# Softmax sums in a decoder kernel: from the exponentials' accumulator to matmuls with a block of ones

## The chip, the cores and the metric

The kernel runs on one core of one Trainium2 chip. The metric is device time of one execution in microseconds (us), as the median of the runs. The engines are TensorE (PE in the rows, its weight loads PEld), VectorE (DVE), ScalarE (ACT), GpSimd (POOL) and the DMA queue of SyncE (SP).

## The reference, cut to what matters

A decoder block on 32 sequences of 128 tokens, width 128, in fp32: a selective state-space layer (scan), then masked attention to a second input with 16 heads of width 8, then a mixture of 8 experts, each followed by a layer norm. The change lies in the attention:

```
scores = jnp.einsum('bnhd,bmhd->bhnm', q, k) / sqrt(8)     # then pad and causal mask
attn = jax.nn.softmax(scores, axis=-1)
out = jnp.einsum('bhnm,bmhd->bnhd', attn, v).reshape(b, s, d)
return out @ Wo.T + bo
```

The softmax is computed as exp(score - max), summed over the keys, and the division is done after the product with the values.

## The kernel before, in words

The 32 sequences go through in G = 8 groups of S = 4. For a group `g` the scan layer runs in a loop of 16 units (`entries` on TensorE, `decay` on ScalarE, `states` on VectorE, `times_c` on GpSimd, `y_add` on TensorE), with pieces of the group before (`w`) and the two after (`e`, `c`) woven in by hand. Behind the loop comes the attention stage of the group, with `t` = 0 to 3 for its four sequences. After the eighth group a routing table is built and 72 expert tiles and a last norm follow. Every engine has one instruction stream, written out in order; an instruction waits on semaphores with `at(engine, name, count)`.

One sequence `t` of the attention stage goes like this.

- `scores(g, t, k)`: TensorE writes the mask and then q times k for 16 heads in four PSUM banks, heads 0 to 7 with k = 0 and 8 to 15 with k = 1 (L1477 the masks, L1484 the products).
- `maxima(g, t, k)`: VectorE takes the negative maxima (L974), two instructions for each half.
- `exps(g, t, k)`: ScalarE takes the exponentials, one instruction for each head, into `prob`, and each also accumulates its row sum into `den` (L692). The trace shows an ACTIVATION_READ_ACCUMULATOR behind each ACTIVATE.
- `head_t(g, t, c)`: TensorE transposes the four heads of block c (L1495) into bank 6 or 7, and `pT_out` copies them to SBUF: c = 0 and 2 on ScalarE (L702), c = 1 and 3 on VectorE (L989).
- `heads_v(g, t)`: 16 matmuls of the transposed exponentials with `v_block` (L1518), in four column blocks of 32, so that head dimensions lie on rows and queries on columns.
- The inverse sums: `inverses` takes the reciprocal of 16 sums for each query (L979), `widen` repeats each 8 times (L983 on VectorE, L706 on ScalarE for t = 3), `inverses_t` transposes the result on TensorE (L1504), it is copied to `rdenT` (L994 on VectorE, L711 on ScalarE for t = 3), and `normed` multiplies (L999) into `aoT`.
- `second_out` projects `aoT` with Wo (L1527, L1529).

`inverses_t(g, t-1)` and `heads_v(g, t-1)` stand in TensorE's stream in turn `t`, between `scores(g, t+1, 0)` and `head_t(g, t, 0)`; those of t = 3 stand behind `entries(e, 1)`. In the turn t = 3 the first two units of the next group are begun: `entries(e, 0)`, `entries(e, 1)`, `decay`, `states(e, 0)` and `states(e, 1)` stand among the last transposes and copies. `entries(e, 2)` stands behind `second_out`, since it writes the bank pair in which `aoT`'s input lies.

Of the kernel before, what the change touches and what calls it, by code (L numbers as in the profile page):

```python
# [8 lines left out]
ALU = mybir.AluOpType  # L9
# [35 lines left out]
def build(nc, a, out):  # L45
    ctx = ExitStack()
    with ctx:
# [20 lines left out]
        sum32 = sb("sum32", [P, 32])  # L68
        diag64 = sb("diag64", [P, HK])
# [66 lines left out]
        rden_wide = sb("rden_wide", [P, 2, P])  # L136
# [3 lines left out]
        den = sb("den", [P, 2, H])  # L140
# [8 lines left out]
        rden = sb("rden", [P, 2, H])  # L149
# [75 lines left out]
        pad_sb mask_sb s_ps s_neg p_sb rden_sb rden_wide_sb pT_ps pT_sb pTd_sb pv_ps rdenT_ps rdenT_sb rdenTd_sb aoT_sb wo_ps  # L225
# [201 lines left out]
        def _(pool):  # L427
# [32 lines left out]
            link(g_.memset(v_block[:, :, :, :], 0.0))  # L460

# [109 lines left out]
        def _(act):  # L571
# [110 lines left out]
            def exps(g, t, k):  # L682
                if t < 2:
                    at(act, "y_sum", 4 * g + 3 + t)
                else:
                    at(act, "pT_ps", 16 * g + 4 * (t - 2) + 2 * k + 2)
                    at(act, "rden_sb", S * g + t - 1)
                for h in range(8 * k, 8 * k + 8):
                    c, j = divmod(h, 4)
                    if j == 0:  # L690
                        at(act, "s_neg", 16 * g + 4 * t + c + 1)
                    last = A(prob[:, t % 2, c, j, :], bank[2 + c][:, j * L:(j + 1) * L], ACT.Exp, bias=nmax[:, t % 2, h:h + 1],  # L692
                             accum_out=den[:, t % 2, h:h + 1])
# [9 lines left out]

            def widen(g, t):
                at(act, "rden_sb", S * g + t + 1)
                A(rden_wide[:, t % 2, :].rearrange("p (h d) -> p h d", h=H), rden[:, t % 2, :].unsqueeze(2).broadcast_to((P, H, HD)),  # L706
                  ACT.Copy).then_inc(s["rden_wide_sb"], 1)

            def rdenT_out(g, t):
                at(act, "rdenT_ps", S * g + t + 1)  # L710
                A(rdenT[:, t % 2], bank[(t + 1) % 2][:, 2 * P:3 * P], ACT.Copy).then_inc(s["rdenT_sb"], 1)  # L711
# [36 lines left out]
            for m in range(G):  # L748
# [55 lines left out]
                for t in range(S):  # L804
                    pT_out(g, t, 0)
                    if t == S - 1:
                        if e is not None:
                            decay(e, 0, range(2))
                        widen(g, t)
                        if e is not None:  # L810
                            decay(e, 0, range(2, NQ))
# [5 lines left out]
                if e is not None:  # L817
                    decay(e, 1, range(2))
                rdenT_out(g, S - 1)
                if e is not None:  # L820
                    decay(e, 1, range(2, NQ))
# [55 lines left out]
        def _(dve):  # L877
# [99 lines left out]
            def inverses(g, t):  # L977
                at(dve, "p_sb", 16 * g + 4 * t + 4)
                v_.reciprocal(rden[:, t % 2, :], den[:, t % 2, :]).then_inc(s["rden_sb"], 1)  # L979

            def widen(g, t):
                at(dve, "rden_sb", S * g + t + 1)
                TT(rden_wide[:, t % 2, :].rearrange("p (h d) -> p h d", h=H), rden[:, t % 2, :].unsqueeze(2).broadcast_to((P, H, HD)),  # L983
                   one_col[:, :].unsqueeze(2).broadcast_to((P, H, HD)), ALU.mult).then_inc(s["rden_wide_sb"], 1)
# [6 lines left out]
            def normed(g, t):  # L991
                if t < S - 1:
                    at(dve, "rdenT_ps", S * g + t + 1)
                    v_.tensor_copy(rdenT[:, t % 2], bank[(t + 1) % 2][:, 2 * P:3 * P]).then_inc(s["rdenTd_sb"], 1)  # L994
                    at(dve, "rdenTd_sb", (S - 1) * g + t + 1)
                else:
                    at(dve, "rdenT_sb", g + 1)
# [77 lines left out]
            for m in range(G):  # L1075
                w, e, c = parts(m)
                g = m
                if w is not None:
                    normed(w, S - 1)
                    second_stats(w, range(S - 1))  # L1080
# [34 lines left out]
                for t in range(S):  # L1115
                    if t == S - 1 and w is not None:
                        ranked(w)
                        normed(g, t - 1)
# [4 lines left out]
                    inverses(g, t)  # L1123
# [646 lines left out]
```

## Time and profile before

| | us |
|---|---|
| median of 3 runs | 1138.08 |
| lowest and highest run | 1131.46, 1140.45 |
| the profiled execution, its own time | 1135.38 |
| span of its profile | 1133.5 |

In the profile PE is busy 962.6 us, ACT 720.5, DVE 697.1 and POOL 576.0. Times in rows are counted from the start of the span. A row of a timeline has the start, the length, the engine, the line and operation, output and inputs, shapes and the count of merged instructions, and in brackets how long the engine was idle before it and what released it. An idle time of 0 is not printed. Lengths overlap: the next instruction of an engine often starts before the modelled end of the one before, so that what one costs is read from start to start.

### The profile page before, as it was taken

The numbers are of one execution on the slowest core, as the hardware profiler recorded it, in microseconds if no ns is written. First come the engines' busy times: TensorE is split into PE (matmuls) and PEld (weight loads), VectorE is DVE, ScalarE is ACT, GpSimd is POOL, SyncE is SP. The second block draws the span as 40 slices with busy tenths as digits, with TensorE's granted clock in tenths as the row PEclk, the third lists the DMA queues.
The fourth block names the chain that finished last, engine by engine and source line by source line (L and its number), as shares of the span: only waits on it lengthen the run. The fifth ranks groups of instructions, "written<-read, shape, count | busy, mean of one in ns | idle before, by whom it ended". The sixth has DMA issues, their size and how long they took to land.

```text
span 1133.5 us, 28078 instructions
## 1 busy us (share of the span) xinstructions
PE 962.6 (85%) x9703; PEld 543.2 (48%) x9704; DVE 697.1 (62%) x1371; ACT 720.5 (64%) x2212; POOL 576.0 (51%) x395
## 2 busy tenths in 40 slices
PE   6799889989788888979888885976937999999997
PEld 2344544444354445435444542543434666666662
DVE  0467667786577767657766794796653544444437
ACT  3567966876696677669667882964822444444446
POOL 2578258457726954782696388268041333333320
PEclk9889999999899999989999996998977999999999
DMA  4606104201500520050042005003131111111134
GB/s 113 138 15 132 30 1 96 66 2 38 133 12 4 124 54 3 17 136 28 4 107 60 4 16 137 2 4 118 50 119 44 41 41 42 42 42 42 42 105 151
DMA packets 69227, 66.69 MB, mean 59 GB/s; under 512 B 9728, under 2 KB 63104, under 8 KB 68736
## 3 DMA queue, kind: packets, MB, share of 16 engines
q1 hardware_dynamic: 63856, 55.59, 19.8%
q0 software_dynamic: 4352, 8.99, 2.4%
q8 instruction: 69, 1.13, 0.4%
q10 hardware_dynamic: 912, 0.67, 0.2%
q14 instruction: 38, 0.31, 0.1%
HBM read 49.09 MB, written 16.13 MB: 58 GB/s over the span
## 4 chain that ended last, share of the span: by engine, by line
PE 45%; POOL 21%; issue 20%; ACT 8%; DVE 5%; DMA 1%; SPq 0%; POOLq 0%; DVEq 0%; ACTq 0%
POOL hst L494 8%; PE pair_a L1682 6%; PE pair_b L1683 6%; PE bank L1696 6%; POOL prob L494 6%; ACT prob L692 5%; POOL xg L526 4%; PE y_ps L1404 3%; PE y_ps L1688 3%; PE pair_b L1484 3%; PE bank L1302 2%; PE y_ps L1484 2%; PE bank L1495 2%; PE pair_a L1518 2%; PE pair_a L1382 1%
## 5 line engine op out<-in xcount | busy, mean ns | idle before, releaser
L651 ACT ACTIVATE decays<-w,a_neg 128x256 f32<-128x256 f32 x512 | 220.5, 509 | 30.2 <-DVE hst L920 17.6
L494 POOL TENSOR_TENSOR hst<-hst,c_rep 128x1024 f32<-128x1024 f32 x64 | 151.4, 2372 | 73.8 <-DVE hst L920 73.1
L494 POOL TENSOR_TENSOR prob<-prob,c_rep 128x1024 f32<-128x1024 f32 x56 | 133.2, 2381 | 57.3 <-DVE prob L920 56.7
L566 POOL DMA_INDIRECT y<-aoT,dest x72 | 69.6, 966 | 173.2 <-DVE aoT L1232 168.8
L920 DVE TENSOR_TENSOR_SCAN prob<-decays,pair_b 128x1024 f32<-128x1024 f32 x32 | 73.1, 2284 | 69.4 <-issue 54.6
L692 ACT ACTIVATE prob<-pair_b,nmax 128x128 f32<-128x128 f32 x256 | 90.4, 399 | 22.4 <-DVE nmax L974 22.3
L1191 DVE TENSOR_TENSOR zpos<-zabs,pair_b 128x512 f32<-128x512 f32 x74 | 50.8, 687 | 81.3 <-PE pair_b L1683 80.2
L1404 PE MATMUL y_ps<-hst,sum 128*32 128x256 f32 x512 | 74.4, 442 | 24.4 <-POOL prob L494 24.4
L692 ACT ACTIVATE prob<-y_ps,nmax 128x128 f32<-128x128 f32 x256 | 90.8, 415 | 0.0
L526 POOL DMA_INDIRECT xg<-x_all,pos x64 | 64.8, 1013 | 35.8 <-DVE pos L1066 23.7
L920 DVE TENSOR_TENSOR_SCAN prob<-decays,pair_a 128x1024 f32<-128x1024 f32 x32 | 73.0, 2281 | 13.5 <-ACT decays L651 9.9
L1682 PE MATMUL pair_a<-w,qk 128*128 x148 | 77.7, 607 | 0.5 <-ACT qk L829 0.5
L1683 PE MATMUL pair_b<-w,qk 128*128 x148 | 76.5, 599 | 0.0
L1696 PE MATMUL bank<-prob,decays 128*128 x576 | 76.1, 275 | 0.0
L1495 PE MATMUL bank<-ident,prob 128*128 128x128 f32 x512 | 70.7, 279 | 5.3 <-ACT pT L702 5.3
L846 ACT ACTIVATE decays<-y_ps 128x512 f32<-128x512 f32 x72 | 43.0, 598 | 50.2 <-PE y_ps L1688 49.5
L1404 PE MATMUL y_ps<-prob,sum 128*32 128x256 f32 x512 | 74.5, 442 | 0.0
L1382 PE MATMUL pair_b<-w,du_tok 64*32 64x256 f32 x2048 | 72.1, 390 | 2.4 <-DVE prob L920 2.3
L486 POOL TENSOR_TENSOR w<-diag,b_tok 128x1024 f32<-128x1024 f32 x32 | 60.6, 1925 | 26.3 <-ACT b_tok L633 26.3
L920 DVE TENSOR_TENSOR_SCAN hst<-decays,pair_b 128x1024 f32<-128x1024 f32 x32 | 72.6, 2270 | 1.6 <-PE pair_b L1382 1.6
L833 ACT ACTIVATE zabs<-pair_a 128x512 f32<-128x512 f32 x74 | 44.2, 597 | 45.4 <-PE pair_a L1682 45.4
L1302 PE MATMUL bank<-xT,w_conv 128*128 128x512 f32 x112 | 62.1, 676 | 10.1 <-ACT xT L581 10.1
(281 smaller groups left out, 2186.0 us busy)
## 6 DMA issues: line engine op xcount, KB each, us to landing
w<-d_dram SPq DMA_DIRECT2D x64, 256.0 KB
c_rep<-c_dram SPq DMA_DIRECT2D x64, 128.0 KB, 3.4
qk<-xg SPq DMA_DIRECT2D x79, 65.0 KB, 1.9
d_dram<-zpos SPq DMA_DIRECT2D x8, 512.0 KB, 3.0
xn<-in_x SPq DMA_DIRECT2D x8, 256.0 KB, 3.0
cn<-in_ctx SPq DMA_DIRECT2D x8, 256.0 KB, 3.3
mask_b<-in_mask SPq DMA_DIRECT2D x8, 256.0 KB, 3.4
w<-in_w1T SPq DMA_DIRECT2D x1, 2048.0 KB, 8.4
```

What stands on the lines that cost most here:

```text
L494: g_.tensor_tensor(by_state(ring(k)), by_state(ring(k)), c_rep[:, :, toks[r]].rearrange("p q (i t) -> p i q t", i=2), ALU.mult).then_inc(s ...
L526: pool.indirect_dma_start(xg[:, :], bass.IndirectOffsetOnAxis(ap=pos[:, t, k:k + 1], axis=0), x2_all[:, w * S + t, :], None).then_inc(s["s ...
L651: last = A(by_state(decays[:, k % 2, :])[:, :, q, :], delta_rep[:, b, toks[r]].rearrange("p (i t) -> p i t", i=2), ACT.Exp, scale=a_neg[:, ...
L692: last = A(prob[:, t % 2, c, j, :], bank[2 + c][:, j * L:(j + 1) * L], ACT.Exp, bias=nmax[:, t % 2, h:h + 1], accum_out=den[:, t % 2, h:h ...
L920: v_.tensor_tensor_scan(ring(k), decays[:, k % 2, :], pair(k)[:, :, :].rearrange("p i c -> p (i c)"), 0.0, ALU.mult, ALU.add).then_inc(s[" ...
L1302: last = MM(bank[b].rearrange("p (s t) -> p s t", s=S), w_conv[:, k, h * P:(h + 1) * P], xT[:, :, k:k + L], start=(k == 0), stop=(k == KCO ...
L1382: last = MM(pair(k)[32 * j:32 * j + 32, i, :].rearrange("p (q y t) -> p q y t", q=NQ, y=2)[:, :, y, :], du_tok[half, r, y, 32 * b:32 * b + ...
L1404: last = MM(y_ps[32 * i:32 * i + 32, r, h * HT:(h + 1) * HT].rearrange("p (i t) -> p i t", i=2), sum32[:, :], by_state(ring(4 * x + i))[:, ...
L1495: last = TR(bank[6 + c % 2][:, j * L:(j + 1) * L], prob[:, t % 2, c, j, :], ident[:, :])
L1682: MM(bank[b], xsT[:, b, :], w1[:, bass.ds(e, 1), :].rearrange("p a f -> p (a f)"), start=True, stop=True).then_inc(s["up_ps"], 1)
L1683: MM(bank[2 + b], xsT[:, b, :], w3[:, bass.ds(e, 1), :].rearrange("p a f -> p (a f)"), start=True, stop=True).then_inc(s["up_ps"], 1)
L1696: last = MM(bank[6][:, b * P:(b + 1) * P], gT[:, b, c, :], w2[:, bass.ds(e, 1), c, :].rearrange("p a d -> p (a d)"), start=(c == 0), stop= ...
```

## The change

The exponentials no longer accumulate. A constant `ones_block` [128, 4, 32] has ones in columns 8j to 8j+7 of block j; `sums_of` multiplies the same transposed exponentials that `heads_v` reads with it, in 16 matmuls of the same shapes, so that each sum stands in PSUM on the 8 rows of its head's values, where `rdenT` wants it. VectorE takes the reciprocal of that 128x128 block straight from PSUM into `rdenT`. `widen`, `inverses_t`, the copy to `rdenT` and the 128x16 reciprocal go, with `den`, `rden` and `rden_wide`. In VectorE's stream `inverses(g, t-1)` now stands directly ahead of `normed(g, t-1)`, that of t = 3 at the start of the next group's loop.

```diff
+        ones_block = sb("ones_block", [P, 4, 32])
...
             link(g_.memset(v_block[:, :, :, :], 0.0))
+            link(g_.memset(ones_block[:, :, :], 0.0))
+            for j in range(4):
+                link(g_.memset(ones_block[:, j, j * HD:(j + 1) * HD], 1.0))
...
# exps (ScalarE)
                     at(act, "pT_ps", 16 * g + 4 * (t - 2) + 2 * k + 2)
-                    at(act, "rden_sb", S * g + t - 1)
...
-                    last = A(prob[:, t % 2, c, j, :], bank[2 + c][:, j * L:(j + 1) * L], ACT.Exp, bias=nmax[:, t % 2, h:h + 1],
-                             accum_out=den[:, t % 2, h:h + 1])
+                    last = A(prob[:, t % 2, c, j, :], bank[2 + c][:, j * L:(j + 1) * L], ACT.Exp, bias=nmax[:, t % 2, h:h + 1])
...
# ScalarE, order of the attention stage
-                    if t == S - 1:
-                        if e is not None:
-                            decay(e, 0, range(2))
-                        widen(g, t)
-                        if e is not None:
-                            decay(e, 0, range(2, NQ))
+                    if t == S - 1 and e is not None:
+                        decay(e, 0, range(NQ))
...
# VectorE
             def inverses(g, t):
-                at(dve, "p_sb", 16 * g + 4 * t + 4)
-                v_.reciprocal(rden[:, t % 2, :], den[:, t % 2, :]).then_inc(s["rden_sb"], 1)
+                at(dve, "den_ps", S * g + t + 1)
+                v_.reciprocal(rdenT[:, t % 2], bank[(t + 1) % 2][:, 2 * P:3 * P]).then_inc(s["rdenT_sb"], 1)
...
                 if w is not None:
+                    inverses(w, S - 1)
                     normed(w, S - 1)
...
-                    inverses(g, t)
-                    if t + 1 < S:
-                        widen(g, t)
                     if t and not (t == S - 1 and w is not None):
+                        inverses(g, t - 1)
                         normed(g, t - 1)
...
# TensorE
-            def inverses_t(g, t):
-                at(pe, "rden_wide_sb", S * g + t + 1)
+            def sums_of(g, t):
+
+                at(pe, "pT_sb", 8 * g + 2 * t + 2)
+                at(pe, "pTd_sb", 8 * g + 2 * t + 2)
                 if t:
                     at(pe, "aoT_sb", S * g + t)
                 else:
                     at(pe, "rotq_sb", 4 * g + 4)
-                TR(bank[(t + 1) % 2][:, 2 * P:3 * P], rden_wide[:, t % 2, :], ident[:, :]).then_inc(s["rdenT_ps"], 1)
+                for j in range(4):
+                    for c in range(4):
+                        last = MM(bank[(t + 1) % 2][32 * c:32 * c + 32, 2 * P:3 * P], ones_block[:, j, :], pT_half[c // 2][:, c % 2, j, :],
+                                  start=(j == 0), stop=(j == 3), skip_group_check=True)
+                last.then_inc(s["den_ps"], 1)
```

## Rows read from the trace of the kernel before

**Rows 1.** The page: busy time by engine, and the chain by engine.

```profile
PE 962.6 (85%) x9703; PEld 543.2 (48%) x9704; DVE 697.1 (62%) x1371; ACT 720.5 (64%) x2212; POOL 576.0 (51%) x395
...
PE 45%; POOL 21%; issue 20%; ACT 8%; DVE 5%; DMA 1%; SPq 0%; POOLq 0%; DVEq 0%; ACTq 0%
```

**Rows 2.** Windows: length, busy PE, PEld, DVE, ACT, POOL, granted clock, DMA share, GB/s.

```profile
408.00:420.00 12.00, 11.47 (x84) 6.14 (x82) 10.34 (x34) 10.14 (x53) 5.13 (x4) 1.00 0.15 44
420.00:431.00 11.00, 9.99 (x84) 5.68 (x83) 8.62 (x21) 10.50 (x54) 1.27 (x1) 1.00 0.11 26
```

**Rows 3.** Timeline of TensorE, attention stage of one group, t = 0 to 2.

```profile
411.05 1.04 PE L1495 MATMUL bank<-ident,prob 128*128 128x128 f32 x8
412.62 0.70 PE L1464 MATMUL pair_a<-aoT,wqT 128*128 128x256 f32 x2 [0.53 <-ACT aoT L680]
...
418.54 0.33 PE L1504 MATMUL pair_a<-ident,rden_wide 128*128 128x128 f32 x1
418.80 0.30 PE L1518 MATMUL pair_a<-pT,v_block 128*32 128x128 f32 x2
...
419.59 0.28 PE L1518 MATMUL pair_a<-pT,v_block 128*32 128x128 f32 x2
...
419.81 1.09 PE L1495 MATMUL bank<-ident,prob 128*128 128x128 f32 x8
420.74 0.59 PE L1477 MATMUL y_ps<-mbias,identb 128*128 128x512 bf16 x2
...
423.25 0.38 PE L1477 MATMUL pair_b<-mbias,identb 128*128 128x512 bf16 x1
423.95 0.39 PE L1477 MATMUL pair_b<-mbias,identb 128*128 128x512 bf16 x1 [0.32 <-ACT prob L692]
424.27 1.13 PE L1484 MATMUL pair_b<-hst,qk 32*128 32x512 f32 x4
...
427.53 0.59 PE L1477 MATMUL y_ps<-mbias,identb 128*128 128x512 bf16 x2
428.05 1.13 PE L1484 MATMUL y_ps<-hst,qk 32*128 32x512 f32 x4
```

**Rows 4.** Timeline of TensorE, the same stage, t = 3 and behind it.

```profile
431.23 0.30 PE L1518 MATMUL pair_a<-pT,v_block 128*32 128x128 f32 x2 [0.91 <-ACT hst L702]
...
434.60 0.63 PE L1495 MATMUL bank<-ident,prob 128*128 128x128 f32 x4 [0.57 <-ACT pT L702]
...
439.39 0.30 PE L1518 MATMUL pair_a<-pT,v_block 128*32 128x128 f32 x2 [1.26 <-issue]
...
441.88 0.46 PE L1527 MATMUL bank<-x1b,ident 128*128 128x128 f32 x2
```

**Rows 5.** Timeline of ScalarE, the same stage.

```profile
411.80 0.40 ACT L692 ACTIVATE prob<-y_ps,nmax 128x128 f32<-128x128 f32 x1
412.05 0.24 ACT L692 ACTIVATION_READ_ACCUMULATOR prob<-y_ps,nmax 128x1 f32 x1
412.14 0.42 ACT L680 ACTIVATE aoT<-pair_a 128x256 f32<-128x256 f32 x1
...
433.75 0.71 ACT L702 ACTIVATE pT<-bank 128x512 f32<-128x512 f32 x1
```

**Rows 6.** Timeline of VectorE, end of the stage and start of the next group.

```profile
430.42 0.68 DVE L989 COPY hst<-bank 128x512 f32<-128x512 f32 x1
...
438.62 0.67 DVE L989 COPY hst<-bank 128x512 f32<-128x512 f32 x1
...
443.75 2.29 DVE L920 TENSOR_TENSOR_SCAN prob<-decays,pair_a 128x1024 f32<-128x1024 f32 x1 [1.04 <-PE pair_a L1382]
```

**Rows 7.** Groups of VectorE by line and shape: busy us, mean ns.

```profile
L979 DVE RECIPROCAL rden<-den 128x16 f32<-128x16 f32 x32 | 8.1, 252 | 9.2 <-ACT prob L692 9.2
...
L1253 DVE RECIPROCAL gates_all<-hst 128x64 f32<-128x64 f32 x1 | 0.6, 553 | 0.0
```

**Rows 8.** Timeline of TensorE, first group, t = 3, answering to 434.60.

```profile
139.45 0.63 PE L1495 MATMUL bank<-ident,prob 128*128 128x128 f32 x4 [1.27 <-ACT pT L702]
```

More of the change, by code:

```diff
@@ L135, in build @@
         rdenT = sb("rdenT", [P, 2, L])
-        rden_wide = sb("rden_wide", [P, 2, P])
         pad = sb("pad", [P, T])
@@ L139, in build @@
         nmax = sb("nmax", [P, 2, H])
-        den = sb("den", [P, 2, H])
         prob = sb("prob", [P, 2, 4, 4, L])
@@ L148, in build @@
                   hst[:, 2, :], hst[:, 3, :], prob_u[:, 2, :], prob_u[:, 3, :]]
-        rden = sb("rden", [P, 2, H])
         aoT = sb("aoT", [P, T])
@@ L224, in build @@
         ln1_stat ln1_var ln1_log ln1_rstd x1_sb x1b_sb x1T_ps x1T_sb cT_ps cT_sb k_ps rotk_sb k_sb k_heads_sb v_ps v_sb q_ps rotq_sb q_sb
-        pad_sb mask_sb s_ps s_neg p_sb rden_sb rden_wide_sb pT_ps pT_sb pTd_sb pv_ps rdenT_ps rdenT_sb rdenTd_sb aoT_sb wo_ps
+        pad_sb mask_sb s_ps s_neg p_sb pT_ps pT_sb pTd_sb pv_ps den_ps rdenT_sb aoT_sb wo_ps
         ln2_stat ln2_var ln2_log ln2_rstd x2_sb x2T_ps x2T_sb lg_ps lg_sb route rank_ps pos_sb row_sb scat
@@ L702, in pT_out @@
                 A(pT_half[c // 2][:, 0], bank[6].rearrange("p (j q) -> p j q", j=4), ACT.Copy).then_inc(s["pT_sb"], 1)
[L704 to L711, printed above, removed]
             def x2_in(w):
@@ L817, in _ @@
                 if e is not None:
[L818 to L821, printed above, removed]
+                    decay(e, 1, range(NQ))
                 else:
@@ L977, in inverses @@
             def inverses(g, t):
-                at(dve, "p_sb", 16 * g + 4 * t + 4)
-                v_.reciprocal(rden[:, t % 2, :], den[:, t % 2, :]).then_inc(s["rden_sb"], 1)
[L981 to L984, printed above, removed]
+                at(dve, "den_ps", S * g + t + 1)
+                v_.reciprocal(rdenT[:, t % 2], bank[(t + 1) % 2][:, 2 * P:3 * P]).then_inc(s["rdenT_sb"], 1)
             def pT_out(g, t, c):
@@ L991, in normed @@
             def normed(g, t):
[L992 to L997, printed above, removed]
+                at(dve, "rdenT_sb", S * g + t + 1)
                 at(dve, "pv_ps", S * g + t + 1)
@@ L1122, in _ @@
                         rope_k(e, 0, 0)
-                    inverses(g, t)
-                    if t + 1 < S:
-                        widen(g, t)
                     if t and not (t == S - 1 and w is not None):
+                        inverses(g, t - 1)
                         normed(g, t - 1)
@@ L1143, in _ @@
                 else:
+                    inverses(g, S - 1)
                     normed(g, S - 1)
@@ L1646, in _ @@
                     if t:
-                        inverses_t(g, t - 1)
+                        sums_of(g, t - 1)
                         heads_v(g, t - 1)
@@ L1664, in _ @@
                     entries(e, 1)
-                inverses_t(g, S - 1)
+                sums_of(g, S - 1)
                 heads_v(g, S - 1)
```

## The prediction

> **What bounds the kernel now.** I read the page first. TensorE is busy 85% of the span and stands for 45% of the chain that ended last, ScalarE for 8% [rows 1]. That says where to look but not what an attention stage is worth, so I took the windows of one stage next. From 408 to 420 us TensorE is busy 11.47 of 12.00 us and ScalarE 10.14, from 420 to 431 us they are busy 9.99 and 10.50 of 11.00, at full granted clock [rows 2]. Both are nearly full, so the question is which one the other waits for. The timeline of TensorE answers it: between 411 and 428 us it is idle twice, 0.53 us for a copy of ScalarE and 0.32 us for an exponential [rows 3]; in t = 3 it waits 0.91, 0.57 and 1.26 us [rows 4]. One turn, from the masks at 420.74 to those at 427.53, takes 6.79 us with only 0.32 us of it idle [rows 3]. So TensorE's own stream sets the length of the turns, and ScalarE is just behind it. The stages of all eight groups show the same pattern; I work on the one at 401 to 444 us.
>
> The exit of the stage matters as well. `entries(e, 2)` stands behind `second_out` in TensorE's stream, and VectorE's scan at 443.75 waits 1.04 us for it [rows 6]. What the stage loses up to there, the next group's loop inherits, since its later units wait for that scan in turn.
>
> **The change part by part.**
>
> ScalarE loses 64 accumulator reads in a group. An ACTIVATE at 411.80 is followed by its read at 412.05 and the next ACTIVATE at 412.14 [rows 5]: 0.34 us for one exponential, 0.09 us of it for the read. A half of 8 exponentials falls from 2.74 us to about 2.0. The bounds are 0.25 us for each (the read alone goes) and 0.34 (nothing gained); I take 0.25. That is 5.9 us less for each group on ScalarE, but only what TensorE waited for counts. Ahead of the queries, the copy at 412.14 starts 0.74 us earlier. TensorE can use it only from the end of its eight transposes: eight take 0.93 us (419.81 to 420.74), so those of 411.05 are through at 411.98, and 412.62 becomes 411.98, a gain of 0.64 us [rows 3]. The wait at 423.95 goes: from 423.25 to the product at 424.27 it was 1.02 us, without a wait 0.52 us (427.53 to 428.05) [rows 3], a gain of 0.50.
>
> TensorE loses `inverses_t`, 0.26 us from start to start (418.54 to 418.80), and gains 16 matmuls of the same shapes as `heads_v` [rows 3]. Those are eight steps, the first at 418.80 and the eighth at 419.59, 0.113 us a step, and the next work starts at 419.81, 1.01 us after the first. Sums and values follow each other in one layout, so I take the eight steps, 0.90 us, and leave the longer last step to `heads_v`; the bounds are 0.90 and 1.01. Net a turn costs 0.64 us more. In t = 1 and t = 2 nothing hides it, because TensorE had no other idle time there. Up to the scores at 428.05 the balance is -0.64 + 0.64 - 0.50 + 0.64 = +0.14 us.
>
> The longer last step of a layout is the trace's own; the Trainium skill (TensorEngine Tiling (Array Packing), Tiling Modes) says that changing the tiling mode drains TensorE, and the rows agree with it (0.22 us for the last step against 0.113). By this rule the sums cost 0.90, without it 1.01, which would be 0.44 us more a group.
>
> In t = 3 the wait moves. Before, `inverses_t` fitted into the 0.91 us that `heads_v` waited for ScalarE's copy [rows 4]. ScalarE's copy comes early now, but VectorE's copy of block 3, at 430.42 for 0.68 us [rows 6], ended only 0.1 us ahead of the old start at 431.23, and it follows the scores and maxima; with the +0.14 from above it is what `sums_of(g, 2)` waits for. So sums start about 0.1 us after the old `heads_v`, and the values 0.90 us after that: +1.0. The next wait, 0.57 us at 434.60 [rows 4], was for a copy that ScalarE began at 433.75, straight behind its last exponential [rows 5]. ScalarE is free sooner now and follows its transposes instead, which start 1.0 us later; I take 0.2 us of the wait back. `entries(e, 0)`, `states(e, 0)` and all behind them come 0.8 us late.
>
> At the end, `heads_v(g, 3)` at 439.39 waited for VectorE's copy at 438.62, which stands behind `states(e, 0)` [rows 4, 6]. `sums_of(g, 3)` waits for the same copy and then puts its 0.90 us ahead of `heads_v`; the transpose that it replaces cost nothing there. `second_out` and `entries(e, 2)` come 0.8 + 0.9 = 1.7 us late.
>
> VectorE takes a reciprocal of 128 instead of 16 columns. 16 took 252 ns and 64 took 553 ns [rows 7], 6.27 ns a column, so 128 from PSUM should take 0.252 + 112 x 0.00627 = 0.95 us; the bounds are 0.68 us, the copy of 512 columns [rows 6], and twice 0.553, 1.1 us. The reciprocal of 16 (0.25), the widening and the copy that go were of nearly the same sum for t under 3, and VectorE has room in the turns. For t = 3 it is new on the path: after the copy (now 439.4), the scan's 2.2 us, the reciprocal 0.95 and the product 0.27 the result is there at about 443.5; TensorE asks for it at 441.88 + 1.7 = 443.6 [rows 4]. It is covered by 0.1 us. Queued behind the waiting reciprocal are `normed`, the statistics of the second norm and `states(e, 2)`; who waits is `second_out`. If the reciprocal takes 1.1 us, 0.05 us a group is added.
>
> The wait on `rden_sb` that `exps` loses and VectorE's wait for the exponentials' end, 9.2 us in 32 reciprocals [rows 7], were short, and what is late next is TensorE; I cost them at nothing. The five memsets at the start stand on GpSimd behind the constant that the others wait for; nothing. `decay(e, 0)` in one piece saves ScalarE a widening of some tenths, but `states(e, 0)` waits for TensorE's entries at about the same time; nothing.
>
> Sum: seven groups at +1.7 us. In the first group the wait that answers to 434.60 was 1.27 us, 0.7 more [rows 8], so it loses 1.0. Together +12.9 us. Against the profiled execution's own 1135.4 that is 1148.3; the median of the runs is 2.7 us higher, 1151.0. I forecast 1150.
>
> **The rivals.**
>
> *Not slower: the exponentials carried the stage.* If TensorE's records overstate what a stream of small matmuls occupies, the sums slip into gaps, and only ScalarE's gain stays: 0.64 + 0.50 + 0.57 = 1.7 us a group, some 14 us, 1124. For it speaks that ScalarE was busy 10.50 of 11.00 us where TensorE was at 9.99 [rows 2]; against it that starts, not modelled ends, give TensorE's 6.79 us turn with 0.32 idle.
>
> *Absorbed.* The stage ends 1.7 us late, but the loop has its own waits behind it and takes half of them up: +6 us, 1143. For it: GpSimd has 21% of the chain [rows 1]. Against it: GpSimd's work there starts with the scans, which are late as well.
>
> *Slower by more: the reciprocal at t = 3 decides.* From about 1.05 us on, every tenth goes onto the path in each of eight groups; with sums at 1.01 us at all four places (+0.44) and a reciprocal of 1.2 us, a group loses 2.3 us, 18 in all, 1156.
>
> *The change does not do what it says.* The reads might not have cost ScalarE anything. Then the 0.64 and 0.50 stay unrecovered: up to 9 us more, 1159. The 0.09 us from start to start speaks against it.
>
> **How the numbers follow.** My forecast has 0.54 (1145 to 1155), the exponentials' rival 0.09, absorbed 0.20 (1139 to 1146), the reciprocal 0.13, reads that were free 0.04. Leaving out the first rival and the ends of the others gives 1141 to 1158. About 1% is what a measurement of this kernel can tell from no change: 1149.5. Of my forecast a little over half lies above it, with the last two 0.50; faster by over 1% is the first rival, 0.09; the rest, 0.41, is within 1%.
>
> **What would show it.** In the changed kernel: ACTIVATEs of L692's successor 0.25 us apart with no reads; sums of 0.90 us; turns of about 7.1 us without a wait for an exponential; TensorE in t = 3 released by VectorE's copy, not ScalarE's; a reciprocal of 0.95 us; the scan of unit 2 later against the start of the stage by 1.7 us. The prediction is wrong if turns stay at 6.5 us, if the next loop is shorter than before by what the stage lost, or if TensorE's clock falls in the stage.

## The result, and the profile after

The changed kernel takes 1151.42 us (median of 4 runs, 1150.45 to 1152.15), the kernel before beside it 1137.64 (4 runs, 1131.46 to 1140.45). The ratio of the runs is 1.0128, 95% interval 1.0086 to 1.017: slower. The profiled execution took 1151.3 us with a span of 1148.6, against 1135.38 and 1133.5 before; the mean granted clock of TensorE is 0.951 in both.

The page of the changed kernel, busy time and the chain, beside [rows 1]:

```profile
PE 982.9 (86%) x10695; PEld 565.7 (49%) x10696; DVE 712.9 (62%) x1323; ACT 671.1 (58%) x1684; POOL 575.6 (50%) x400
...
PE 50%; POOL 21%; issue 20%; DVE 4%; ACT 3%; DMA 1%; SPq 0%; POOLq 0%; DVEq 0%; ACTq 0%
```

ScalarE is busy 49 us less, TensorE 20 us more. ScalarE's share of the chain falls from 8 to 3%, TensorE's rises from 45 to 50%. These shares name what lies on one chain of work, and do not tell what the change is worth.

The windows of the same stretch of the same stage, beside [rows 2]:

```profile
413.00:425.00 12.00, 12.00 (x115) 6.79 (x114) 10.53 (x33) 8.04 (x29) 5.17 (x4) 1.00 0.16 46
425.00:436.00 11.00, 10.45 (x115) 6.43 (x114) 8.24 (x17) 8.67 (x30) 1.27 (x1) 1.00 0.11 25
```

TensorE has no idle time left in the first window (11.47 us busy before), and ScalarE now has 3.96 us of slack in it.

TensorE's timeline, the stage that answers to [rows 3, 4] (every group of 16 matmuls is cut to its first and last rows):

```profile
416.17 1.04 PE L1469 MATMUL bank<-ident,prob 128*128 128x128 f32 x8
...
423.05 0.30 PE L1482 MATMUL pair_a<-pT,ones_block 128*32 128x128 f32 x2
...
423.84 0.28 PE L1482 MATMUL pair_a<-pT,ones_block 128*32 128x128 f32 x2
...
423.94 0.28 PE L1498 MATMUL pair_a<-pT,v_block 128*32 128x128 f32 x2
...
424.93 1.09 PE L1469 MATMUL bank<-ident,prob 128*128 128x128 f32 x8
...
431.84 1.09 PE L1469 MATMUL bank<-ident,prob 128*128 128x128 f32 x8
...
436.45 0.30 PE L1482 MATMUL pair_a<-pT,ones_block 128*32 128x128 f32 x2 [0.99 <-ACT hst L701]
...
440.46 0.63 PE L1469 MATMUL bank<-ident,prob 128*128 128x128 f32 x4 [0.34 <-ACT pT L701]
...
445.25 0.30 PE L1482 MATMUL pair_a<-pT,ones_block 128*32 128x128 f32 x2 [1.52 <-issue]
...
446.12 0.31 PE L1498 MATMUL pair_a<-pT,v_block 128*32 128x128 f32 x2
...
447.13 0.91 PE L1507 MATMUL bank<-x1b,ident 128*128 128x384 f32 x2
...
448.66 0.46 PE L1507 MATMUL bank<-x1b,ident 128*128 128x128 f32 x2
```

The sums take 0.89 us (423.05 to 423.94), the values behind them 0.99 with the longer last step (423.94 to 424.93). A turn takes 6.91 us (424.93 to 431.84) and no wait for an exponential is left in it. The Trainium skill (TensorEngine Tiling (Array Packing), Tiling Modes) says that a change of tiling mode drains TensorE. The two figures agree with it: only the second of two groups in one layout pays the longer step. At t = 3 the row at 436.45 names ScalarE's `hst` as releaser, but the copy of ScalarE was begun at 435.05 and took 0.63 us. The VectorE copy in the next fence ended at 436.34, and that is what the sums waited for.

VectorE's timeline of the end of that stage, beside [rows 6]:

```profile
435.66 0.68 DVE L967 COPY hst<-bank 128x512 f32<-128x512 f32 x1
...
442.28 2.29 DVE L903 TENSOR_TENSOR_SCAN hst<-decays,y_ps 128x1024 f32<-128x1024 f32 x1 [0.87 <-ACT decays L652]
444.48 0.67 DVE L967 COPY hst<-bank 128x512 f32<-128x512 f32 x1
445.06 2.28 DVE L903 TENSOR_TENSOR_SCAN hst<-decays,pair_b 128x1024 f32<-128x1024 f32 x1
447.25 0.94 DVE L962 RECIPROCAL rdenT<-pair_a 128x128 f32<-128x128 f32 x1
448.22 0.29 DVE L972 TENSOR_TENSOR aoT<-pair_a,rdenT 128x128 f32<-128x128 f32 x1
...
450.53 2.29 DVE L903 TENSOR_TENSOR_SCAN prob<-decays,pair_a 128x1024 f32<-128x1024 f32 x1 [1.09 <-issue]
```

The same engine and place in the kernel before, with the three rows that [rows 6] leaves out:

```profile
436.42 2.29 DVE L920 TENSOR_TENSOR_SCAN hst<-decays,y_ps 128x1024 f32<-128x1024 f32 x1 [1.62 <-PE y_ps L1382]
...
439.26 2.29 DVE L920 TENSOR_TENSOR_SCAN hst<-decays,pair_b 128x1024 f32<-128x1024 f32 x1
441.47 0.27 DVE L999 TENSOR_TENSOR aoT<-pair_a,rdenT 128x128 f32<-128x128 f32 x1
```

In both kernels VectorE goes from the scan straight to what follows it. Before, that was the product. Now the reciprocal stands between them, and the product comes 5.94 us after the scan of unit 0 (442.28 to 448.22), where it came 5.05 us after it (436.42 to 441.47). The last part of `second_out` at 448.66 starts when the product is done at 448.51. The reciprocal is therefore on the path, which the prediction had denied; e3, e4 and e7 test it.

The groups by line, beside [rows 7]:

```profile
L962 DVE RECIPROCAL rdenT<-pair_a 128x128 f32<-128x128 f32 x32 | 30.3, 946 | 2.5 <-PE pair_a L1482 2.5
```

From such starts I made a ledger for every kernel below. A group's stage is cut at the first maxima of t = 1, the last maxima of t = 3, the scan of unit 0 and the scan of unit 2 of the next group. For each stretch I take the kernel's length minus that of the kernel before. The figures are those of the second to seventh group, which agree within 0.05 us but for the exit of e5, given as a range, and the turns of e2's fourth group (-0.98); the first group differs and is named where it counts. The last column is the last group alone, from its last maxima to the start of its last product. In the stage shown the whole is 32.70 us before and 34.36 after (the starts of the scan of unit 2 less those of the first transposes of t = 0: 443.75 - 411.05 and 450.53 - 416.17), +1.66.

| kernel | turns | to unit 0 | to unit 2 | last group's exit |
|---|---|---|---|---|
| changed kernel | +0.12 | +0.62 | +0.92 | +2.19 |
| e1, accumulation kept | +1.21 | +0.63 | +0.92 | +2.22 |
| e2, before without accumulation | -1.11 | -0.26 | 0.00 | -0.16 |
| e3, a quarter of the sums | -1.20 | -0.01 | +0.92 | +0.91 |
| e4, copy for the reciprocal | +0.12 | +0.61 | +0.74 | +1.59 |
| e5, e3 and e4 together | -1.18 | -0.01 | +0.25 to +0.35 | +0.34 |
| e6, t = 3 the old way | +0.13 | +0.64 | 0.00 | +1.40 |
| e7, output ahead of the sums | +0.13 | +0.62 | +0.92 | +2.62 |
| e8, before in another order | -0.31 | -0.02 | 0.00 | +0.92 |

In the changed kernel six groups lose 1.66 us each, the first 0.84 and the last 2.19: 13.0 us, where the medians differ by 13.8. The stretches between the stages differ too, from the scan of unit 2 to the first maxima of t = 1: by -1.65 to +3.86 us in a single one, +4.7 together, and what lies ahead of the first stage is 2.6 us shorter. The balance, +2.1, is what is left of the spans' difference of 15.1; behind the last stage there is nothing. That part I come back to with e6 and e10.

### The profile page after: what moved, and what is told of

The parts are those of the page before. It is cut to its first block, busy times and chain, and to the rows that moved or that the text cites. A ratio compares the mean times of both kernels' runs of the same rounds, so it can differ in the third digit from the quotient of the medians.

```text
span 1148.6 us, 29477 instructions
## 1 busy us (share of the span) xinstructions
PE 982.9 (86%) x10695; PEld 565.7 (49%) x10696; DVE 712.9 (62%) x1323; ACT 671.1 (58%) x1684; POOL 575.6 (50%) x400
## 4 chain that ended last, share of the span: by engine, by line
PE 50%; POOL 21%; issue 20%; DVE 4%; ACT 3%; DMA 1%; SPq 0%; POOLq 0%; DVEq 0%; ACTq 0%
POOL hst L495 8%; POOL prob L495 6%; PE pair_a L1662 6%; PE bank L1676 6%; PE pair_b L1663 6%; POOL xg L527 4%; PE bank L1469 4%; PE pair_b L1458 3%; PE y_ps L1378 3%; PE y_ps L1458 3%; PE y_ps L1668 3%; PE bank L1276 2%; PE pair_a L1482 2%; PE pair_a L1498 1%; PE pair_a L1398 1%
## 5 line engine op out<-in xcount | busy, mean ns | idle before, releaser
L652 ACT ACTIVATE decays<-w,a_neg 128x256 f32<-128x256 f32 x512 | 217.4, 498 | 36.5 <-DVE hst L903 23.8
L692 ACT ACTIVATE prob<-pair_b,nmax 128x128 f32<-128x128 f32 x256 | 69.6, 398 | 24.2 <-DVE nmax L957 24.2
L1676 PEld LDWEIGHTS bank<-prob,decays 128*128 128x128 f32 x576 | 70.0, 192 | 0.0
```

Of the source, the lines that this page charges most:

```text
L652: last = A(by_state(decays[:, k % 2, :])[:, :, q, :], delta_rep[:, b, toks[r]].rearrange("p (i t) -> p i t", i=2), ACT.Exp, scale=a_neg[:, ...
L1676: last = MM(bank[6][:, b * P:(b + 1) * P], gT[:, b, c, :], w2[:, bass.ds(e, 1), c, :].rearrange("p a d -> p (a d)"), start=(c == 0), stop= ...
```

## The experiments

Each ratio is to the kernel before as it ran beside it: 1135.86 us for e1 to e4, 1132.62 for e5 to e8, 1135.42 for e9 to e12.

**e1: the accumulation kept.** The changed kernel with the accumulator back in the exponentials, whose result nothing reads.

```diff
-                    last = A(prob[...], bank[2 + c][...], ACT.Exp, bias=nmax[:, t % 2, h:h + 1])
+                    last = A(prob[...], bank[2 + c][...], ACT.Exp, bias=nmax[:, t % 2, h:h + 1],
+                             accum_out=den[:, t % 2, h:h + 1])
```

> The changed kernel with the accumulation left in the exponentials (the sums it makes are not read). TensorE sets the turns, by my account: a turn of the changed kernel takes 6.91 us (424.93 to 431.84) and ScalarE, which idles 1.7 us in it, needs 8 x 0.09 us twice more, 1.48 us, so turns t = 1 and 2 stay as they are. What comes back is the 0.64 us ahead of the queries in t = 0, and in t = 3 at most 0.1 us at the sums of t = 2 and nothing at the 1.98 us idle before the copy for block 0. +0.7 us a group, +5 to 6 us on 1151.4: 1157. Rival, ScalarE paces the stage: all 64 reads of 0.09 us count, +5.9 us a group, 1198. Rival, the reads were free: 1151.

1157.59 us (4 runs), ratio 1.0197 (1.0175 to 1.0219). The turns go from +0.12 to +1.21: the reads cost 1.09 us a group (1.2 in the first and the last), where 0.7 was expected. TensorE's timeline shows where, and a row of ScalarE's the start of the chain:

```profile
419.77 0.70 PE L1440 MATMUL pair_a<-aoT,wqT 128*128 128x256 f32 x2 [0.52 <-ACT aoT L682]
...
431.71 0.39 PE L1453 MATMUL pair_b<-mbias,identb 128*128 128x512 bf16 x1 [0.31 <-ACT prob L693]
```

```profile
428.27 0.60 ACT L703 ACTIVATE pT<-bank 128x512 f32<-128x512 f32 x1 [1.01 <-PE bank L1471]
```

The wait at the queries, 0.52 us, is that of [rows 3], as expected. The wait for an exponential at the second masks is there as well, 0.31 us, though the turn has become longer by the sums. I had thought that a longer turn gives ScalarE the time for it. It does not, because this wait is a chain and not a matter of room. ScalarE waits 1.01 us for the transposes, copies at 428.27, takes eight exponentials at 0.34 us, and the mask follows at 431.71. The chain starts at the transposes, behind the sums, so it moves with them.

**e2: the kernel before without the accumulation.** The sums are not computed; the output is divided by a constant 64.

```diff
+            link(g_.memset(den[:, :, :], 64.0))
-                             accum_out=den[:, t % 2, h:h + 1])
```

> The kernel before without the accumulation in the exponentials; the sums are a constant 64 instead, so the division is by a constant. This is the change's gain alone. By my terms: 0.64 us ahead of the queries, 0.50 us at the masks of t = 2, 0.2 us at the copy in t = 3, nothing at the end: 1.34 us a group, 10.7 us in all, 1137.6 - 10.7 = 1127. The copy of VectorE that follows the scores moves with them, so the 1.14 us should survive the wait of the values of t = 2. Rival, ScalarE paces the stage: up to 5.9 us a group, 1090. Rival, free reads: 1137.

1126.8 us (4 runs), ratio 0.9914 (0.9897 to 0.9931). The stage is 1.37 us shorter, 1.11 of it in the turns, beside 1.34 expected (the 0.64 and 0.50 at two waits of [rows 3], and what is left at t = 3). This is the gain half of the change by itself, 9.1 us by the medians and 11.7 by the ledger over eight groups (2.19 in the first). It also shows that the exponentials' rival was wrong: had ScalarE carried the stage, more would be gained, for it is relieved by 5.9 us a group.

**e3: a quarter of the sums.** Four of 16 matmuls stay; the sums of the other 12 blocks are left out. `ones_block` is filled with ones, so that no sum is zero.

```diff
-            link(g_.memset(ones_block[:, :, :], 0.0))
+            link(g_.memset(ones_block[:, :, :], 1.0))
...
-                for j in range(4):
+                for j in (0,):
...
-                                  start=(j == 0), stop=(j == 3), skip_group_check=True)
+                                  start=True, stop=True, skip_group_check=True)
```

> The changed kernel with 4 of the 16 matmuls of each sums block (12 left out, so that only a quarter of the sums is right in kind). Two of eight steps stay, 0.11 us each: 0.66 us less on TensorE at each of four places. By my account t = 1, t = 2 and the sums of t = 2 give 0.66 us each, 2.0 us a group; at the end of the stage VectorE's reciprocal takes over, since it ends at 448.22 where TensorE's second part starts at 448.66 (0.15 us of cover), so the fourth place gives only some 0.15 us. 2.1 us a group, 17 us: 1134.5. If all four places counted in full: 2.6 us a group, 1130. Rival, the sums fit into gaps and something else is slower: 1151.

1135.85 us (10 runs), ratio 0.9998 (0.9984 to 1.0011). The turns fall by 1.32 (from +0.12 to -1.20, two groups of sums at 0.66), the stretch to unit 0 by 0.63, as expected. The exit does not fall at all: +0.92 with 16 matmuls, +0.92 with four. VectorE's and TensorE's timelines of this kernel:

```profile
437.74 2.28 DVE L903 TENSOR_TENSOR_SCAN hst<-decays,pair_b 128x1024 f32<-128x1024 f32 x1
439.93 0.93 DVE L962 RECIPROCAL rdenT<-pair_a 128x128 f32<-128x128 f32 x1
440.90 0.29 DVE L972 TENSOR_TENSOR aoT<-pair_a,rdenT 128x128 f32<-128x128 f32 x1
```

```profile
437.92 0.30 PE L1482 MATMUL pair_a<-pT,ones_block 128*32 128x128 f32 x2 [1.52 <-issue]
...
439.29 0.91 PE L1507 MATMUL bank<-x1b,ident 128*128 128x384 f32 x2
...
441.33 0.46 PE L1507 MATMUL bank<-x1b,ident 128*128 128x128 f32 x2 [0.47 <-DVE aoT L972]
```

TensorE is through early and waits 0.47 us for the product. From the scan of unit 1 on the exit is set by scan, reciprocal, product, and no matmul stands between them. I had expected 0.15 us to come back here.

**e4: a copy in the reciprocal's place.** The sums are computed, but the division by them is left out: `rdenT` gets the sums themselves.

```diff
-                v_.reciprocal(rdenT[:, t % 2], bank[(t + 1) % 2][:, 2 * P:3 * P]).then_inc(s["rdenT_sb"], 1)
+                v_.tensor_copy(rdenT[:, t % 2], bank[(t + 1) % 2][:, 2 * P:3 * P]).then_inc(s["rdenT_sb"], 1)
```

> The changed kernel with a copy of the 128x128 block (0.28 us) in place of the reciprocal (0.95 us): the division is left out, it multiplies by the sums. By my account the reciprocal is covered by 0.15 us in the first seven groups, so nothing changes there; in the last group, which has no scans behind it, it stands on the path twice (ahead of the copy for block 1 in t = 3 and ahead of the last product): -0.7 to -1.3 us in all, 1150. Rival, the reciprocal decides: 0.67 us in each of eight groups or more, 1146 or lower.

1145.18 us (4 runs), ratio 1.0102 (1.0056 to 1.0148). VectorE's timeline of this kernel:

```profile
443.49 2.27 DVE L903 TENSOR_TENSOR_SCAN hst<-decays,pair_b 128x1024 f32<-128x1024 f32 x1
445.68 0.26 DVE L962 COPY rdenT<-pair_a 128x128 f32<-128x128 f32 x1
445.98 0.29 DVE L972 TENSOR_TENSOR aoT<-pair_a,rdenT 128x128 f32<-128x128 f32 x1
```

VectorE is done 0.67 us sooner (0.97 against 0.30 from the reciprocal's or copy's start to the product's), and the stage gains 0.18 of it, where I had expected nothing: from +0.92 to +0.74. The rest is not gained, because TensorE's stream, with its sums, then comes last. So the two engines are 0.18 us apart at the exit, with VectorE behind. Over seven groups, and 0.60 in the last, that is 1.9 us. The ratios to the kernel before differ by 0.26%, 3 us, and the medians, taken beside different runs of the kernel before, by 6. The interval of this ratio is wide (0.9 of a per cent), so I read the price of the reciprocal from the ledger and not from the medians.

**e5: both.** The edits of e3 and e4 together.

> The changed kernel with both: 4 of 16 matmuls of the sums, and a copy in place of the reciprocal (12 sums of 16 and the division are left out). With TensorE 0.66 us shorter at the end of the stage, the reciprocal is what second_out waits for; the copy takes it away again. Against the quarter of the sums alone: 0.5 us less in each of seven groups and more in the last, -4 us: 1130.5. Rival, the fourth place had counted in full already: no difference from the quarter alone.

1135.15 us (10 runs, one of them of 5187.7 us, which the ratio leaves out; the median of the other nine is 1133.72), ratio 1.0015 (0.9986 to 1.0043). The exit falls to +0.25 to +0.35: with e3 alone it was +0.92, with e4 alone +0.74. Only with both terms gone does it move by more than 0.18, as two branches that end nearly together must behave. The median is not the 1130.5 that I expected. The ledger gives it 5.0 us less than e3 over eight groups, for the 4 expected, but the nine runs of this one kernel lie from 1127.2 us at a mean granted clock of 0.953 over 1133.7 at 0.945 to 1140.6 at 0.938; one of 1140.0 at 0.91 falls out of that line.

**e6: the last sequence the old way.** New sums for t < 3; for t = 3 the accumulator, the reciprocal of 16 columns, the widening, the transpose and the copies.

```diff
+                    if t == S - 1:
+                        last = A(..., ACT.Exp, bias=..., accum_out=den[:, h:h + 1])
...
+            def inverses_old(g):
+                at(dve, "p_sb", 16 * g + 16)
+                v_.reciprocal(rden[:, :], den[:, :]).then_inc(s["rden_sb"], 1)
...
             def inverses(g, t):
-                at(dve, "den_ps", S * g + t + 1)
+                if t == S - 1:
+                    return
+                at(dve, "den_ps", (S - 1) * g + t + 1)
```

> A mixture that computes the reference: t = 0 to 2 by matmuls as in the changed kernel, t = 3 as before (accumulation, 128x16 reciprocal, widening, transpose). The sums ahead of the last values cost 0.92 us a group by the trace of the changed kernel, where the old transpose stood in idle time. Against that the exponentials of t = 3 take 1.5 us longer on ScalarE; the idle 1.98 us before the copy for block 0 covers them, and the copy that the sums of t = 2 wait for comes at most 0.1 us later. The widening puts 0.2 us into the decays of unit 0. -0.6 to -0.9 us a group: 1151.4 - 6 = 1145. Rival: what is saved at the end is lost to the longer exponentials, 1151.

1150.62 us (4 runs), ratio 1.0159 (1.0134 to 1.0184): a miss. The ledger shows what I meant to get, the exit back at 0.00 in seven groups and 1.40 in the last, in all 6.9 us less than in the changed kernel. The time shows none of it. What is worse is the clock. In every trace TensorE is granted one of two levels, 2.4 and 1.2 GHz, so with a mean of 0.939 over a span of 1149.0 us it is at the lower one for 2 x 0.061 x 1149.0 = 140 us. The changed kernel has 2 x 0.049 x 1148.6 = 113, the kernel before 111. The three other runs have 0.942 to 0.944. The window over the eight groups, e6 alone (the granted clock is the third column from the end; the changed kernel has 0.95 there):

```profile
45.00:820.00 775.00, 664.98 (x8644) 358.03 (x8642) 546.95 (x750) 518.02 (x1429) 473.79 (x277) 0.94 0.22 54
```

The stretches between the stages show where it went. These are two of them, that behind the stage shown and the next, first in the kernel before, then in the changed kernel, then in e6:

```profile
443.75:511.46 67.71, 56.78 (x675) 27.27 (x675) 45.31 (x60) 43.70 (x109) 52.40 (x32) 0.95 0.29 71
544.34:612.11 67.77, 57.00 (x675) 27.14 (x675) 45.33 (x60) 43.71 (x109) 52.38 (x32) 0.95 0.28 68
```

```profile
450.53:517.10 66.57, 55.31 (x675) 26.64 (x675) 45.32 (x60) 42.95 (x98) 52.14 (x31) 0.97 0.31 73
551.63:619.38 67.75, 56.95 (x675) 27.21 (x675) 45.34 (x61) 42.96 (x98) 52.14 (x31) 0.95 0.29 68
```

```profile
449.41:519.84 70.43, 59.66 (x675) 28.12 (x675) 47.96 (x60) 43.05 (x98) 52.19 (x32) 0.90 0.29 68
553.49:622.66 69.17, 59.29 (x675) 27.90 (x675) 46.59 (x60) 43.09 (x98) 52.18 (x32) 0.90 0.27 66
```

Where the granted clock is the same (0.95), the kernel before and the changed one take the same time, 67.77 and 67.75 us. At 0.97 it is 66.57, at 0.90 it is 69.17 and 70.43. In e6 all that lies outside the stages is 7.5 us longer than in the changed kernel, 5.3 of them in these two stretches, against the 6.9 that its stages gain. So in the profiled execution the gain was lost where the clock was lower. That the clock is the cause of that length and not only goes with it is not tested by e6. That it can cost that much is seen in e5 too, where 0.015 of clock goes with 13.4 us.

**e7: the output ahead of the last sums.** The three first parts of `second_out` stand ahead of `sums_of(g, 3)` in TensorE's stream, so that only one stands behind the last values.

```diff
+                at(pe, "pT_sb", 8 * g + 8)
+                second_out(g, range(S - 1))
                 sums_of(g, S - 1)
                 heads_v(g, S - 1)
-                second_out(g, range(S - 1))
                 second_out(g, (S - 1,))
```

> The changed kernel with second_out of t = 0 to 2 moved ahead of the sums and values of t = 3 (it computes the reference). TensorE idles 1.52 us there and this work takes 1.5 us, so TensorE would reach the second part 1.5 us sooner; but the product with the inverses is ready only at 448.5, against 448.66 now. So the reciprocal is what is late next and only 0.15 us a group comes back, -1 us: 1150. Rival, TensorE's stream alone decides the exit: -1.5 us a group, 1139.

1149.73 us (4 runs), ratio 1.0145 (1.0121 to 1.0169). The exit stays at +0.92, as in e3: less TensorE work behind the sums is worth nothing while VectorE's chain is later. TensorE now waits 1.46 us for the product, which is done at 447.94, and starts 0.15 us behind that. The last group pays 0.43 more.

**e8: the kernel before in another order.** `inverses_t` behind `heads_v`, and the same move of `second_out`, to see whether order alone is worth something without the change.

```diff
-                        inverses_t(g, t - 1)
                         heads_v(g, t - 1)
+                        inverses_t(g, t - 1)
...
+                at(pe, "pT_sb", 8 * g + 8)
                 second_out(g, range(S - 1))
+                heads_v(g, S - 1)
-                heads_v(g, S - 1)
```

> The kernel before (it computes the reference) with two pieces of TensorE's stream in another order: inverses_t(g, t-1) behind heads_v(g, t-1), next to other 128-column transposes, 0.12 instead of 0.26 us, and second_out of t = 0 to 2 ahead of the last values. The first saves 0.14 us in t = 1 and 2, but ScalarE is nearly as full as TensorE before (two halves of exponentials and two copies are 6.46 us of 6.79), the second at most 0.1 us, since the product with the inverses is ready at 441.75 and is asked for at 441.88. -0.1 to -0.4 us a group: 1137.6 - 2 = 1135, within what can be told. Rival: the transposes behind the values delay the product that the next values wait for, +0.3 us a group.

1132.46 us (12 runs), ratio 0.9991 (0.9975 to 1.0007): no difference. The turns gain 0.31 us and the last group loses 0.92. The exit of the other seven stays at 0.00, and TensorE's timeline tells what sets it in the kernel before:

```profile
439.79 0.46 PE L1527 MATMUL bank<-x1b,ident 128*128 128x128 f32 x2 [1.41 <-DVE aoT L999]
```

With three parts of the output out of the way TensorE waits 1.41 us for the product, and the stage is no shorter for it. The product, done at 439.65, was already what the exit hung on without the change.

**e9: two orders in the kernel before.** The first edit of e8 in the turns, and on ScalarE `dtl_out(e, 5)` ahead of `ln_scale2(w)`.

```diff
                         if k == 2:
+                            if e is not None:
+                                dtl_out(e, 5)
                             ln_scale2(w)
...
-                        if k == 2:
+                        if k == 2 and w is None:
                             dtl_out(e, 5)
```

> The kernel before (it computes the reference) with two other orders: inverses_t behind heads_v in t = 1 to 3, which gave 0.31 us a group up to the scores of t = 3 in the run before; and dtl_out ahead of ln_scale2 on ScalarE at unit 2. TensorE waits 1.22 us at 447.74 for that copy, which stands behind the logarithm that waits for VectorE's statistics (446.67) while its own input is there at 445.5; the chain of TensorE from 447.74 to 458 leads to the convolution that the scan at 463.49 waits for. If that chain sets the scan, 1.2 us in each of six groups, -7 us, and with the 0.31 us -9.5 us: 1125. If VectorE's own stream, full from 443.75 to 459.4, takes it up, only the -2.5 us stay: 1132.

1126.09 us (5 runs), ratio 0.9921 (0.9903 to 0.9939). The idea is from the loop and not from the stage. In the kernel before, ScalarE waits for the norm's variance with the copy that TensorE needs queued behind it:

```profile
446.67 0.30 ACT L664 ACTIVATE lnv<-mv,eps_col 128x4 f32<-128x4 f32 x1 [3.32 <-DVE mv L1010]
...
447.11 0.58 ACT L612 ACTIVATE dtl<-y_ps 128x512 f32<-128x512 f32 x1
```

In e9 the copy goes first, as soon as TensorE's product is there, and the variance behind it:

```profile
441.84 0.60 ACT L612 ACTIVATE dtl<-y_ps 128x512 f32<-128x512 f32 x1 [2.19 <-PE y_ps L1321]
442.97 0.30 ACT L664 ACTIVATE lnv<-mv,eps_col 128x4 f32<-128x4 f32 x1 [0.54 <-DVE mv L1012]
```

From the scan of unit 2 to that of unit 8, at the same clock, it is 1.3 to 1.6 us shorter in six groups (25.44 for 26.80 us where the clock fell in it, 23.86 for 25.16 where it did not), and the turns 0.30: near 10 us, of which 9.3 arrive in the medians. In this trace alone two of the six are 0.3 us longer, because the clock fell in them and had not in the kernel before.

**e10 and e11: TensorE kept busy ahead of the stage.** In both kernels TensorE idles just before its attention stage, until GpSimd has the queries' products. Here are the rows of the kernel before:

```profile
399.73 1.67 PE L1484 MATMUL pair_b<-hst,qk 32*128 32x512 f32 x4 [3.47 <-POOL qk L499]
401.33 0.64 PE L1404 MATMUL y_ps<-hst,sum 128*32 128x256 f32 x2
...
401.76 0.64 PE L1404 MATMUL y_ps<-hst,sum 128*32 128x256 f32 x2
```

Behind 3.47 us of idle time the steps are 0.43 us, at a granted clock of 0.57 in the window from 399.7 to 403.4; from 403.75 on they are 0.22. The edit puts 13 idle matmuls into that gap, in e10 in the kernel before, in e11 in the changed one.

```diff
+            def warm(g):
+                if g + 1 < G:
+                    at(pe, "duT_sb", 2 * g + 4)
+                keep_warm(13, 6)
...
+                if k == 0 and t == 0:
+                    warm(g)
```

> The kernel before (it computes the reference) with 13 idle 128x128 matmuls into bank 6 between the first masks of the stage and the wait for the queries, where TensorE idles 3.5 to 4.4 us and the granted clock falls to its half level in some groups (400.2 to 403.6 us of the trace). If the clock then holds, y_add of the last units runs in 0.21 instead of 0.42 us a step: up to 2 us a group in those groups where the clock fell, -5 to -12 us: 1126; and the spread of the loops between kernels should shrink. If the clock falls for other reasons, no change: 1134.

> The changed kernel with the same 13 matmuls. The change's price in the stages is 1.66 us a group in six, 0.84 in the first and 2.2 in the last by the traces, 13 us; with the clock alike in both it should stand against the kernel before with the same matmuls undisturbed: its time + 13 us, a ratio of 1.0115 between the two. Rival: part of the 13 to 15 us between the kernels was the clock, and the ratio is under 1.008 or over 1.015.

e10 took 1126.39 us (6 runs), ratio 0.992 (0.9901 to 0.9939); e11 took 1141.40 (5 runs), ratio 1.0066 (1.0047 to 1.0086). In e10 the stretch from the first maxima of t = 0 to those of t = 1 is 1.1 to 1.9 us shorter in five groups (up to 0.45 longer in the others), and the mean granted clock of the two profiled executions is 0.961 and 0.965. The pair tells more than either alone. It is the change with fewer of the clock's falls: TensorE is at the lower level for some 89 and 79 us, for 111 and 113 without the matmuls. The medians are 15.0 us apart (1.0133, where 1.0115 was expected), the two profiled executions 11.5, and in the ledger of e11 stand the same +0.12, +0.61 and +0.92. Stage by stage e11 loses 13.3 us against e10. Outside the stages that pair of traces differs by -1.8 us, in stretches where the clock differs again. In two stretches where it is the same the difference is 0.03 us and less. The cost of the change is thus in the stage, whatever the clock does ahead of it; the 1.7 us by which the medians' 15.0 exceeds the ledger are not explained.

**e12: the kernel before with e9 and e10.** This computes the whole of the reference.

> The kernel before (it computes the reference) with both orders and the 13 matmuls: if the three act in different places, the sum of their gains, 1117 to 1122. If both act on the same wait, as the better of the two.

1114.13 us (5 runs), ratio 0.9819 (0.9795 to 0.9842). It beats both kernels, by no less than the sum of its parts (1.8% beside 0.79 and 0.80). TensorE's timeline ahead of a stage:

```profile
388.74 3.06 PE L1455 MATMUL bank<-ident 128*128 128x128 f32 x26
392.89 1.13 PE L1493 MATMUL pair_b<-hst,qk 32*128 32x512 f32 x4 [1.08 <-POOL qk L499]
393.94 0.41 PE L1406 MATMUL y_ps<-hst,sum 128*32 128x256 f32 x2
...
394.19 0.39 PE L1406 MATMUL y_ps<-hst,sum 128*32 128x256 f32 x2
```

The gap is 1.08 us in place of 3.47, and the steps behind it are 0.25 and then 0.21 us from the start.

## Why the prediction was right, and where it was not

The forecast of 1150 is 1.4 us below the 1151.42, which its range holds. The sum of the steps, 12.9 us, meets the 13.0 of the ledger. That the medians' 13.8 lies so near is in part luck: the stretches outside the stages, forecast at nothing, differ by up to 3.86 us each and come to +2.1 in the spans. Step by step:

- *ScalarE's gain, 0.64 and 0.50 us.* Right. e2 has 1.11 us in the turns, e1 takes back 1.09. The wait at the queries and that at the masks are gone in the changed kernel. The sign given for it, turns of about 7.1 us, did not follow from these terms: 6.79 + 0.64 - 0.50 is 6.93, and 6.91 was measured.
- *The sums, 0.90 us in two turns.* Right: 0.89, and the turns' balance is +0.12 for +0.14. e3 shows the price of a matmul step by taking 12 of 16 away.
- *t = 3: sums released by VectorE's copy, +0.8 to the next group's states.* The releaser is as foretold, the size 0.74 (0.12 + 0.62). The answering wait kept 0.34 of its 0.57 us, so 0.23 was taken back for the 0.2 assumed.
- *The exit, +0.9 by the sums ahead of the last values, the reciprocal "covered by 0.1 us".* This is the step that failed, and that its size came out right is luck: two branches end within 0.18 us of each other. The exit's +0.92 is VectorE's. Its product starts 0.89 us later against the scan of unit 0 (5.94 for 5.05), in a chain that already set the exit before (e8). TensorE's sums alone would give +0.74 (e4). The reciprocal is late by 0.18 us, not early by 0.1. Three quarters of the sums taken away at this place gain nothing (e3), nor does the output moved ahead of them (e7).

  The prediction's chain was well timed: its 443.5 holds the copy's length of some 0.6 us, which its list of terms leaves out, and in the kernel before's time the product is done at 443.4 (448.51, less the 5.12 us by which this stage starts later). What it had wrong was the time to hold that against. It took 441.88 for the moment at which TensorE asks, but that start was already set by the product, done at 441.74, and a hand-over of some 0.15 us (448.51 to 448.66 in the changed kernel, the same in e3, e7 and e8). TensorE's own stream had some 0.13 us to spare there: from the six matmuls of the output to the entries it takes 1.34 us before (441.15 to 442.49) and 1.20 in e4 (446.31 to 447.51), where nothing holds it up. So its 0.87 us of sums (445.25 to 446.12) push the exit by 0.74 only, while VectorE's new term counts nearly in full. The price is 0.18 us in seven groups and 0.60 in the last, 1.9 us of 13.
- *The reciprocal's duration, 0.95 us.* Right: 946 ns. The estimate from the Trainium skill (VectorE: DVE Perf Modes, First, the fixed hardware budget), about 1.2 us for 128 columns, is not borne out.
- *First group +1.0, the others +1.7.* 0.84, six at 1.66, and the last at 2.19, where no work of a next group stands beside the sums: 1.28 us go when 12 of the 16 matmuls do (e3), 0.60 with the reciprocal (e4), 1.85 with both (e5).

Of the rivals, that the exponentials carried the stage falls by e2 and by the turns without a wait. "Absorbed" falls as well: at the same granted clock the stretch behind a stage is as long in the changed kernel as before (67.75 and 67.77 us), so it gives nothing back of the 1.66. "The reciprocal decides" was right about the place and wrong about the size, as it is 0.18 us ahead of the other branch and no more. That the reads were free falls by e1.

What is open: why the changed kernel and e6 fall to the lower clock in other places than the kernel before. The stretches outside the stages scatter by up to 4 us each with it, and what e6 gains in its stages is lost there. e11 against e10 shows that the stage's cost does not hang on it.

## What to carry to other kernels

Work taken from one engine is worth only the waits of the others that end with it: here 49 us of ScalarE bought 9 to 12 us in all (e2), and the 20 us of TensorE put in its place cost more than that. When two engines end together at the exit of a stage, follow both chains in the trace, and take work away from each in turn, then from both, before naming the one that carries it. And compare the granted clock of two kernels before their times, since a gain of half a per cent in the stages can vanish in it.

## What the runs showed of the hardware

- An accumulator output costs ScalarE a read of its own, 0.09 us from start to start for a 128x128 exponential from PSUM (0.34 to 0.25), and on TensorE's path 1.09 us a group for 64 of them (e1).
- A reciprocal of 128 columns from PSUM takes 0.946 us, a copy of the same block 0.26 to 0.28 (e4).
- Sixteen matmuls in four column blocks go in eight steps of 0.113 us; the last step is 0.22 when a 128x128 matmul follows.
- The two stretches shown with e6 take 66.57 us at a granted clock of 0.97, 67.71 to 67.77 at 0.95 and 69.17 to 70.43 at 0.90. At 0.95 the kernel before and the changed one do not differ.
- One kernel's time moves with the mean granted clock: eight of nine runs of e5 lie between 1127.2 us at 0.953 and 1140.6 at 0.938, the slower the lower the clock, give or take 2 us; the ninth took 1140.0 at 0.91. An idle time of 3.47 us ahead of a stage went with 0.57 of the clock in the next 3.7 us. Thirteen matmuls in the gap, which compute nothing, made the kernel before 0.8% faster.
